# Adding a wait to GpSimd's scatters: not until the second to last has landed

## The reference

```python
scores = x @ router_w.T + router_bias            # 16 experts
topv, topi = top_k(scores, 2);  weights = softmax(topv)
mag, freq = x @ bank_mag[n], x @ bank_freq[n]    # 128 -> 256, for expert n
hidden = tanh(mag) * cos(softplus(freq) + 0.1 + bank_phase[n])
out = sum over the two picks of weight * (hidden @ bank_down[n])
out = out * rsqrt(mean(out * out) + 1e-6) * norm_w
```

## Time and profile before

| what | value |
|---|---|
| median of 3 runs | 710.82 us (706.82 to 713.89) |
| profiled execution, its own time | 708.06 us |
| its span, first to last instruction | 706.3 us |
| mean granted TensorE clock | 0.821 of full speed |
| busy shares | PE 64%, DVE 67%, ACT 48%, POOL 58% |
| second layer's scatters (line 564) | from 595.17 to 684.4 us, 47 of them |
| results loaded back | from 685.84 us on |

### The profile page before, as it was taken

One profiled execution on the slowest core, in us unless ns is written; L12 is line 12 of the kernel. 1 busy time (PEld: TensorE's weight loads), 2 busy tenths in 40 slices (PEclk: granted clock), 3 DMA queues, 4 the chain that ended last, 5 costly groups with the idle time before them and its releaser, 6 DMA issues.

```text
span 706.3 us, 8200 instructions
## 1 busy us (share of the span) xinstructions
PE 455.1 (64%) x2131; PEld 307.3 (44%) x2131; DVE 472.8 (67%) x908; ACT 336.4 (48%) x655; POOL 406.6 (58%) x317
## 2 busy tenths in 40 slices
PE   3655975988797577736787786269540488686520
PEld 2322422433333233525776676126530387486410
DVE  5958899899999999761333223648534567567817
ACT  3165864584586364212222225374310089579805
POOL 0029999899899899116666654512575102545850
PEclk9886999899999899756789999569555599989765
DMA  5053556545345351014566573300012455443125
GB/s 185 0 177 108 180 183 189 164 149 179 120 141 175 121 178 45 20 50 141 185 192 202 180 218 104 110 0 1 19 53 89 168 187 191 160 143 138 46 66 153
DMA packets 58382, 90.21 MB, mean 128 GB/s; under 512 B 7569, under 2 KB 32658, under 8 KB 58338
## 3 DMA queue, kind: packets, MB, share of 16 engines
q1 hardware_dynamic: 52162, 78.88, 34.2%
q0 software_dynamic: 5024, 10.30, 4.9%
q10 hardware_dynamic: 1152, 0.52, 0.3%
HBM read 66.21 MB, written 11.14 MB: 110 GB/s over the span
## 4 chain that ended last, share of the span: by engine, by line
PE 18%; issue 11%; DVE 10%; POOL 7%; another core or an unknown queue 6%; ACT 4%; DMA 2%; SPq 1%; DVEq 1%; POOLq 0%; ACTq 0%
POOL y_dram L564 6%; PE ps L1298 5%; PE ps L1287 4%; PE ps L1107 2%; PE ps L1456 1%; PE ps L1338 1%; PE ps L1165 1%; DMA xl<-x_slots 1%; DMA y_dram<-ys,rows_i 1%; DMA y1b<-y_dram 1%; ACT h_tok L904 1%; PE ps L1330 1%; SPq L516 1%; DVE ht L1896 1%
## 5 line engine op out<-in xcount | busy, mean ns | idle before, releaser
L593 POOL TENSOR_TENSOR bu<-uT,b_sb 128x1024 f32<-128x1024 f32 x64 | 153.3, 2419 | 29.5 <-DVE uT L1796 29.5
L564 POOL DMA_INDIRECT y_dram<-ys,rows_i x86 | 93.6, 1089 | 114.8 <-DVE ys L2063 64.8
L1165 PE MATMUL ps<-prod,cst 128*128 128x512 f32 x256 | 127.9, 647 | 37.5 <-DVE yT L1840 18.2
L776 ACT ACTIVATE ps<-dtT,neg_a 128x512 f32<-128x512 f32 x128 | 83.2, 681 | 41.1 <-DVE prod L1820 29.1
L1165 PEld LDWEIGHTS ps<-prod,cst 128*128 128x128 f32 x256 | 50.4, 204 | 107.0 <-issue 77.4
L604 POOL TENSOR_TENSOR prod<-hs,c_sb 128x1024 f32<-128x1024 f32 x28 | 67.2, 2399 | 13.3 <-DVE hs L1810 7.8
L882 ACT ACTIVATE ht<-ps,b1T 128x128 f32<-128x128 f32 x78 | 24.5, 366 | 82.8 <-PE ps L1287 43.9
L1298 PE MATMUL ps<-w_s,ht 128*128 x312 | 47.2, 299 | 25.3 <-issue 11.7
L1456 PE MATMUL ps<-xt,mfr 128*128 128x128 f32 x376 | 52.8, 295 | 9.0 <-issue 3.8
L1298 PEld LDWEIGHTS ps<-w_s,ht 128*128 128x128 f32 x312 | 41.9, 209 | 30.8 <-issue 30.8
L1456 PEld LDWEIGHTS ps<-xt,mfr 128*128 128x128 f32 x376 | 49.1, 208 | 12.4 <-issue 9.7
(11 more groups left out here) (293 smaller groups left out, 904.9 us busy)
## 6 DMA issues: line engine op xcount, KB each, us to landing
b_sb<-b_rows SPq DMA_DIRECT2D x32, 512.0 KB
c_sb<-b_rows SPq DMA_DIRECT2D x32, 512.0 KB
mfr<-mf_s SPq DMA_DIRECT2D x47, 256.0 KB
w1r<-in_w SPq DMA_DIRECT2D x39, 256.0 KB
mf_s<-in_mf SPq DMA_DIRECT2D x16, 256.0 KB
xl<-x_slots SPq DMA_DIRECT2D x47, 64.0 KB
w_s<-in_w SPq DMA_DIRECT2D x9, 256.0 KB, 4.5
down_s<-in_down SPq DMA_DIRECT2D x16, 128.0 KB
```

The costliest lines, as they stand in the source:

```text
L564: pool.indirect_dma_start(y_dram[l], bass.IndirectOffsetOnAxis(ap=rows_i[:, 1, j:j + 1], axis=0), ys[:, j % slots, :], None).then_inc(save ...
L593: nc.gpsimd.tensor_tensor(bu[:, g % RING, :, :], uT[:, c % 2, :, :], b_sb[:, k % BRING, g % 2, :].unsqueeze(1).broadcast_to([P, ND, CHUNK] ...
L776: nc.scalar.activation(decay_of(g, d), dtT[:, c % 2, d, :], ACT.Exp, scale=neg_a[:, d, n:n + 1]).then_inc(S["a_ready"], 1)
L1165: last = nc.tensor.matmul(bank(Y_BANK + d), ident, prod[:, g % RING, d, :], start=n == 0, stop=n == NS - 1)
```

## The change

`put_rows` gets a third wait. For the second layer (l = 1) and the tiles 2 to 35, GpSimd also waits until tile j - 2 has landed, before it issues the scatter of tile j. `LAST_UP` = 24 - 6 = 18 is the first pair of the last quarter, so tiles 36 to 46 are without it, and the first layer is untouched.

```diff
 MR = 4
+IN_FLIGHT = 2
+LAST_UP = NPAIR - QP
 LN_EPS = 1e-5
...
                 if slots > XR and j >= XR:
                     pool.wait_ge(saved[u], 16 * (rounds(l, u) + j // XR))
+                if l and IN_FLIGHT <= j < 2 * LAST_UP:
+                    before = j - IN_FLIGHT
+                    pool.wait_ge(saved[before % XR], 16 * (rounds(l, before % XR) + before // XR + 1))
                 pool.indirect_dma_start(y_dram[l], bass.IndirectOffsetOnAxis(ap=rows_i[:, 1, j:j + 1], axis=0),
                                         ys[:, j % slots, :], None).then_inc(saved[u], 16)
```

## The result

| | before | after |
|---|---|---|
| median of 20 runs each | 711.93 us (703.64 to 719.35) | 703.45 us (698.24 to 716.04) |
| span of the profiled execution | 706.3 us | 700.4 us |
| mean granted TensorE clock | 0.821 | 0.808 |

The change adds waits only, and still something went faster.

What follows compares the result with a forecast made beforehand. GpSimd's scatters were taken to bound the kernel from tile 24 (651.78 us) to the end. The mean of four executions, 709.9 us, plus 0 for crowding and 1.36 for the added waits gave 711.3 us, range 706 to 717.

Steps and rivals of the forecast that it cites:

- the crowding: All bursts: two scatters never move at once, so a limit of two spares the DMA engines nothing; 0 us.
- The fast rival: First burst: crowded scatters make TensorE stutter and spacing them ends it; up to 1.6 us earlier; chance 0.12.
- at most 0.48 more: Extra spacing the wait puts between scatters, given against the fast side; at most 0.48 us.
- The added wait: Third burst, tiles 26 to 35: waits for landings start the last scatter 1.36 us later, range 0.4 to 2.4.
- price: Each wait: landing 1.28 us after GpSimd's end on a tile, then 0.76 to the next start, 2.04 together.
- the quiet 1.28: Third burst, quiet DMA engines: a scatter lands 1.28 us after GpSimd is done with it.
- The cover: Idle 10.61 and 6.86 us ahead of tiles 12 and 24 hide the first two bursts' delays, 1.23 and 1.58.
- The slow rival: Third burst, tiles 26 to 35: the wait becomes the bound; 12.6 us at landings of 2.8, 7.1 at 2.3; chance 0.08.
- my upper end of 2.8: Landing under load, from tile 22 in the second burst: at most about 2.8 us after GpSimd's end.
- the recurrence: Tile j starts at the later of tile j-1's end + 0.30 and tile j-2's end + landing + 0.76.

Runs made afterwards that it cites:

- f1: Kernel before plus four chained memsets ahead of each scatter of tiles 2 to 23, no wait for a landing; ratio to before 0.9844.
- e3: Changed kernel with its added waits on a semaphore reached long before, so they hold nothing back; ratio to the kernel before 0.9974.
- f2: Kernel before plus two chained memsets ahead of each scatter of tiles 2 to 23, no wait for a landing; ratio to before 0.9841.
- f3: The changed kernel again, unedited, on a chip where the kernel before stutters; ratio to before 0.9812.
- f0: The kernel before, unedited, profiled again in the last group; bursts 16.0 and 15.2 us, pair 9 to last scatter 87.1 us.
- e11: The changed kernel again, unedited, on a chip of the first kind; ratio to the kernel before 0.9893.
- e8: Kernel before plus one chained memset ahead of each scatter of tiles 2 to 23, no wait for a landing; ratio to before 0.9913.
- e7: The changed kernel again, unedited, on the chip where the kernel before takes 669.59 us; ratio to before 1.0034.
- e4: Changed kernel with the limit of two in the first two bursts only, tiles 2 to 23, on the 669.59 us chip; ratio to the kernel before 1.0016.
- e6: Kernel before plus one unchained memset ahead of each scatter of tiles 2 to 23, no wait, on the 669.59 us chip; ratio to before 0.9968.
- e0: The kernel before, unedited, profiled once more in the first group; bursts 15.8 and 10.1 us, pair 9 to last scatter 83.2 us.

## Why the prediction was wrong

**The step that failed** is "I cost this at 0", the crowding. Its argument was that two scatters never move at once on the DMA engines, so spacing them spares nobody. That looked for the victim on the wrong resource. The scatters' packets indeed don't overlap, in the busy bursts of the kernel before either (tile 22's, the slowest there, are through by 645.4, and tile 23's begin at 645.56), and TensorE's matmuls come late all the same. What the runs showed in place of the 0 is 8.45 + 3.31 us in the two stretches of the first pair of profiles. Spacing by itself, without any limit (f1), brings the two stretches down to 9.8 as well, and an idle wait (e3) brings nothing.

**The fast rival was mis-sized.** "TensorE is freed" named the right mechanism, its row and even its condition ("crowded scatters cause it, and spacing them ends it"), at 1.6 us and 0.12. In the profiles it was 8.45 + 3.31 = 11.8 us, some of the 3.31 perhaps the clock's. I had added up only the gaps ahead of line 1456. They leave out 0.8 us of the same kind ahead of line 1468 in that window, they show less than half of what TensorE loses, and nothing of what that does to the groups behind it. The right measure is the time that a fixed piece of work takes inside and outside the burst: three pairs 18.2 us in one burst and 13.1 in the other, for the same work. Two such stretches with different times, in the profile of before alone, would have given 5 us for the one burst alone. My argument that the spacing is "at most 0.48 more" was right on the spacing and wrong on its weight: 0.24 more, from 1.26 to 1.50, is nearly enough (f2).

**The added wait: right in sign and price, and right in size in one pair of four.** Predicted was +1.36, all from the third burst, and 0.4 to 2.4 as its range. From tile 24 to tile 36 the limit cost +3.06 us in the first pair of profiles, +1.35 in group 4 (f3 against f0), 2.05 in group 3 (e11 against e8) and 2.2 in group 2 (e7 against e4 to e6). The gaps of 0.78 to 0.80 and the form of the new waits are as forecast. In the first pair the gaps over 0.30 come to 0.48 + 2.06 + 0.90 + 0.50 + 0.49 + 0.49 = 4.92, and the scatters' durations to 13.19 instead of 15.00, 1.8 less; that makes the +3.06 of the burst. Tile 26 alone is 2.06 of it, and there the landing was not the quiet 1.28 (below).

**The cover was wrong.** I had the delays of the first bursts hidden in the idle 10.61 and 6.86. That idle time was there in part because the stutter held up the results; without it pair 15 to pair 21 takes 22.7 us, and twelve scatters under the limit may take longer. GpSimd's timeline in f3, tile 24, whose pair 21 starts at 639.91:

```profile
640.68 0.96 POOL L569 DMA_INDIRECT y_dram<-ys,rows_i  x1 [0.78 <-issue]
```

It starts 0.77 after pair 21, against 653.73 - 655.23 = -1.50 in f0: 2.27 us of lost cover, more than the 1.35 of the third burst. With 0.36 less in tiles 36 to 46 that is the 33.43 - 30.17 = 3.26 of the table. In the first pair the loss of cover is 0.52 (642.74 - 643.72 = -0.98 against 651.78 - 653.28 = -1.50), and 3.06 + 0.52 - 0.36 = 3.22. In e7 and e11 it is nothing (-1.49 and -1.50). The prediction had the condition ("If that cover were gone they would come on top"), with 1.58 at most, and took it as not met. The sequencer no longer runs ahead either: its last separate wait was at 676.6, and the last of the new line is at 662.5, just ahead of its scatter.

**The slow rival** had its place right and did not decide. A landing of 3.34 after the end of GpSimd's work, worse than my upper end of 2.8, did occur, but for one tile and not for all. Its 12.6 and 7.1 us are not of the third burst alone, as it reads: the recurrence gives 8.3 and 5.8 there, and the rest is lost cover.

**The sum.** With the sizes as measured: -11.8 in the bursts, +3.2 at the end, so -8.5 in the layer, against a measured -6.6 in the ratio (between 4.8 and 8.4). The layer began 2.2 us later after than before, and the end took 0.5 longer. The stutter differs from one execution to the next (10.1 to 18.2 us a burst), so a single profile pair may well lie 2 us off. Without the limit in the third burst the layer should gain 1.4 to 3.1 us more; f2's total fits that, its ratio can't tell.

**What stays open.** Why dense scatters hold up TensorE, and why not in each execution and not on each chip. The trace shows bundles each 0.75 us and no wait. The transfers of instructions that it lists (the queues of the kind "instruction") don't explain it: in this layer those of 16 KB take 0.9 to 1.4 us in f0 and in f3 alike, and in f0 none begins between 593.16 and 613.03, while the bundles of burst 1 stand from 602.8 to 609.4. Nor is it told apart whether the number of scatters under way counts beside their pace, since spacing lowers both; the limit of three says only that three are too many at a step of 1.26. A kernel with the same scatters and fewer bytes was not tried.

## What to carry to other kernels

A DMA issuer with slack may be too fast for its neighbours: look at fixed pieces of another engine's work inside and outside its bursts, and take the difference of their times, not the sum of the unexplained gaps, as the bound. If it is real, spread the issues over the idle time that the issuer has (here 0.24 us more a scatter was nearly enough), not over more of it than is left once the neighbour is quick again (f1 and f3 lost 3.0 and 2.3 us that way), and leave the spacing out where the issuer itself is the bound. Read the granted clock of each stretch beside its time. Repeat the profile before believing a size, and on another chip, since the changed kernel gained on three occasions with the kernel before at 711 to 713 us (ratios 0.9907, 0.9893 and 0.9812) and not on the chip at 670 (1.0034).

## What the hardware showed unexpectedly

**Chips differ.** The same kernel before took 711.9, 707.4, 710.7 and 712.9 us on four occasions, and 669.6 on one. There the first expert layer is quicker by far, and the four kernels profiled there had no stutter in the second. All engines in the stretch from 330 to 370 us, a part of the first expert layer that the change doesn't touch; first e0, then e7:

```profile
330.00:370.00 40.00, 29.51 (x211) 27.83 (x212) 14.48 (x53) 9.17 (x36) 23.36 (x25) 0.87 0.61 182
```

```profile
330.00:370.00 40.00, 36.13 (x315) 35.18 (x314) 20.25 (x71) 14.35 (x54) 30.33 (x32) 1.00 0.86 263
```

TensorE's weight loads waited in it like this, in e0 and then in e7 (us in total, times, longest us):

```profile
PEld ps L1298 <- issue: 15.5, 8, 4.5
```

```profile
PEld ps L1292 <- issue: 2.3, 2, 1.8
PEld ps L1303 <- issue: 2.2, 2, 1.8
```

The same kind of unexplained wait, 15.5 us against 4.5. TensorE may be held up there as in the bursts, but the granted clock differs too, 0.87 against 1.00, and no run tells which of the two comes first.

**One instruction transfer held up one scatter.** Tile 26 of the kernel after waited 2.36 us for the landing of tile 24. The DMA queues of the kernel after, 644.6 to 644.7 us and 645.9 to 646.0 us (packets begun, MB, share of 16 engines):

```profile
q8 instruction: 1, 0.02, 84.2%
```

```profile
q0 software_dynamic: 1, 0.00, 1.6%
```

0.842 x 16 x 0.1 us = 1.35 us for one packet of 16 KB, on one of the 16 engines. All but one of tile 24's packets had begun by 644.62; its last, the 4 bytes by which that one engine reports, began at 645.96, when the instruction packet was done. So a scatter that is spread over 16 engines lands when the most hindered one is through, and a limit on landings lets such a transfer show. In e7 the same shows: tile 27 waited 1.66 for the landing of tile 25, with such a packet from 616.74 on. The Trainium skill, "DMA: Bandwidth & Descriptors", Queues, rings and completion order, has an engine drain a whole packet from one queue before it turns to another. The trace agrees: the 4 bytes began only when the 1.35 us of the 16 KB packet were over.
